# Two cross-attentions whose maxima enter the score product, in a fused two-layer decoder

## What is computed

```
scores = einsum('nqhd,nkhd->nhqk', q, k)        # layer 1: divided by sqrt(16)
attn = softmax(scores, axis=3)
out = einsum('nhqk,nkhd->nqhd', attn, v) @ W + b
```

## Time and profile before

| | us |
|---|---|
| median of 3 runs (2005.93 to 2014.84) | 2013.31 |
| the profiled execution, its own time | 2014.15 |
| its span in the trace | 2012.2 |
| TensorE busy (matmul) / weight loads | 1711.1 (85%) / 1349.4 (67%) |
| VectorE / ScalarE / GpSimd busy | 1163.6 (58%) / 622.9 (31%) / 895.1 (44%) |
| mean granted clock of TensorE, share of full | 0.91 |
| layer 0 attention, first product to first shared unit | 27.49 to 577.18 |
| shared units and experts of layer 0 | 577.18 to 1146.9 |
| layer 1 attention to first expert tile | 1146.9 to 1590.5 |
| experts of layer 1 | 1590.5 to 2012.2 |

### The profile page before, as it was taken

The page is one execution under the profiler, slowest core; times in us unless marked ns, Lnnn a source line. Parts: engine busy times, 40 slices in busy tenths (PEclk is TensorE's granted clock), DMA queues, the critical chain, the costliest instruction groups (busy, mean ns, idle before and its releaser), DMA issues.

```text
span 2012.2 us, 45539 instructions
## 1 busy us (share of the span) xinstructions
PE 1711.1 (85%) x17739; PEld 1349.4 (67%) x17739; DVE 1163.6 (58%) x3228; ACT 622.9 (31%) x957; POOL 895.1 (44%) x1000
## 2 busy tenths in 40 slices
PE   3788888888789899998998478899987499999994
PEld 2676666666656566665666345676656499999994
DVE  3576655755532176776656456787765345665554
ACT  0233222332221176544455123354432011111110
POOL 0006557556758201888888856333322201222223
PEclk9999978988679999999999678999887699999997
DMA  9415434545457899987999922113101512333332
GB/s 320 147 36 195 161 133 159 171 145 173 164 171 215 224 289 299 297 271 252 296 299 305 301 78 83 54 65 129 63 33 50 169 49 75 92 95 93 101 92 69
DMA packets 269634, 322.61 MB, mean 160 GB/s; under 512 B 25083, under 2 KB 245487, under 8 KB 268655
## 3 DMA queue, kind: packets, MB, share of 16 engines
q1 hardware_dynamic: 236399, 227.38, 35.7%
q0 software_dynamic: 33024, 92.32, 14.1%
HBM read 157.22 MB, written 162.40 MB: 159 GB/s over the span
## 4 chain that ended last, share of the span: by engine, by line
PE 60%; DVE 11%; POOL 8%; issue 7%; DMA 5%; ACT 3%; another core or an unknown queue 3%; SPq 1%; DVEq 1%; POOLq 0%; ACTq 0%
PE wide L2039 13%; PE d_yp L2051 6%; POOL big L1413 5%; PE wide L1171 4%; PE wide L1174 3%; PE wide L110 3%; PE wide L127 3%; PE bank L1191 3%; PE wide L1158 2%; PE bank L1184 2%; PE bank L1005 2%; PE bank L1148 2%; ACT pt L650 2%; PE bank L1077 2%
## 5 line engine op out<-in xcount | busy, mean ns | idle before, releaser
L1413 POOL DMA_INDIRECT big<-results,slots x256 | 268.4, 1048 | 207.0 <-DMA results<-e_y 127.3
L2039 PE MATMUL wide<-d_xt,d_ws 128*128 128x128 f32 x2272 | 278.4, 276 | 0.6 <-issue 0.6
L2039 PEld LDWEIGHTS wide<-d_xt,d_ws 128*128 128x128 f32 x2272 | 272.1, 193 | 4.5 <-issue 1.0
L588 POOL DMA_INDIRECT lists<-big,slots x160 | 159.1, 994 | 118.5 <-DVE slots L940 72.1
L650 ACT ACTIVATE pt<-wide 77x2048 f32<-77x2048 f32 x64 | 119.9, 1873 | 210.9 <-PE wide L1174 126.7
L1908 POOL DMA_INDIRECT d_picked<-results,slots x64 | 63.8, 997 | 181.5 <-DMA results<-d_y 168.2
L1939 ACT ACTIVATE d_gate<-wide 128x512 f32<-128x512 f32 x71 | 42.4, 597 | 324.6 <-PE wide L2039 320.0
L1428 DVE SCALAR_TENSOR_TENSOR big<-big,weights 128x256 f32<-128x256 f32 x256 | 108.9, 486 | 51.9 <-DMA big<-results,slots 33.9
L2051 PE MATMUL d_yp<-d_wd,d_h 128*128 x568 | 134.2, 379 | 0.0
L110 PE MATMUL wide<-shared_sx,shared_sw 128*128 128x512 f32 x256 | 127.0, 619 | 6.3 <-DMA shared_sx<-res_t 3.8
L127 PEld LDWEIGHTS wide<-shared_sw,shared_sh 128*128 128x128 f32 x512 | 99.8, 196 | 46.3 <-issue 29.9
(11 more groups left out here) (280 smaller groups left out, 3528.3 us busy)
## 6 DMA issues: line engine op xcount, KB each, us to landing
lists<-zero SPq DMA_DIRECT2D x20, 2048.0 KB, 14.4
e_x<-lists SPq DMA_DIRECT2D x80, 512.0 KB
results<-e_y SPq DMA_DIRECT2D x80, 512.0 KB
d_x<-lists SPq DMA_DIRECT2D x71, 128.0 KB
results<-d_y SPq DMA_DIRECT2D x71, 128.0 KB
e_w<-in_L_w SPq DMA_DIRECT2D x2, 4096.0 KB
x<-in_x SPq DMA_DIRECT2D x8, 512.0 KB
shared_sw<-in_x_t SPq DMA_DIRECT2D x32, 128.0 KB
```

What stands on the lines that cost most here:

```text
L588: pool.indirect_dma_start(out=lists, out_offset=bass.IndirectOffsetOnAxis(ap=slots[:, b, i, k:k + 1], axis=0), in_=z2[i % 3][:, b, :], in_ ...
L1413: pool.indirect_dma_start(out=picked[:, c % NG, b, :], out_offset=None, in_=results[0:-(-PAGES_OF_STEP[s] // 4) * 4 * R0, :], in_offset=ba ...
L2039: ins = mm(out[T % 2][:, a * P:(a + 1) * P], ws[:, T % NW, n, c, a * P:(a + 1) * P], xt[:, T % 2, c], start=c == 0, stop=c == KC - 1)
```

## The change

1. The maxima are laid out differently. peak is now [128, batch, chunk, 128], and the negated maximum of a head stands in the column of one channel of the *other* head of its pair. mt has two jobs a step (a pair of batches each) of four transposes; their result has the maxima in rows that the masked copy of the queries leaves at zero.
2. ScalarE makes, beside the plain copy of the transposed queries (x1t in layer 0, q in layer 1; semaphore qt_done), two masked copies `split[:, a]` with mask2 as scale. VectorE's part of mt adds the maxima into the other rows of each: `split = maxima * mask2[other] + split`.
3. keys_max is a second set of keys with ones (sel_at) added in the row of the maxima. sc is one product, keys_max x split, where it was two. `sel` is gone; mx keeps keys and the plain queries.
4. SEQUENCE0 and SEQUENCE1 are new orders, with other distances between stages (in layer 0 v, kt, ret, mix, mx, sc, x2t one round later relative to qk, for instance; b2's halves in two rounds).
5. Layer 0: x_t is loaded first, then eight constants on their own semaphore consts_soon, then x and the rest. TensorE starts after consts_soon; it waits for the others before ("wo", 0, 0) and for the tables (READY, now 31) before ("mx", 0, 0). VectorE makes the retention's tables first and the others (`lay_out`) when it reaches ("mx", 0, 0). Layer 1: context, wk and wv are loaded first, and ten loads (`others`) are issued from ScalarE's queue; the tables are still made before the first job.

```
-SEQUENCE0, stages in the order before: wo, wo, put, v, v, ln1, wout, wout, cwt, put, qk,
-  x1t, x1t, mx, ln2, qk, b2, b2, mx, res, put, qk, x2t, x2t, mx, put, qk, mx, put, kt, ret, kt, put, mt, rt, put, put,
-  sc, mix, top, ret, pv, sc, mix, up, rank, sc, pv, sc, pv, pv
+SEQUENCE0 = [
+    ("mx", 2, 1), ("x1t", 2, 1), ("put", 4, 2), ("up", 2, 0), ("mx", 2, 2), ("b2", 4, 1), ("v", 1, 0), ("mx", 2, 3),
+    ("kt", 1, 0), ("mt", 2, 0), ("ret", 1, 0), ("ln2", 3, 0), ("mt", 2, 1), ("v", 1, 1), ("x2t", 3, 0), ("x2t", 3, 1),
+    ("ret", 1, 1), ("kt", 1, 1), ("rt", 3, 0), ("put", 4, 3), ("put", 4, 4), ("top", 3, 0), ("mix", 1, 0), ("put", 4, 5),
+    ("mix", 1, 1), ("put", 4, 6), ("wo", 1, 0), ("wo", 1, 1), ("put", 4, 7), ("rank", 3, 0), ("res", 2, 0), ("cwt", 3, 0),
+    ("qk", 0, 0), ("sc", 2, 0), ("qk", 0, 1), ("sc", 2, 1), ("pv", 2, 0), ("sc", 2, 2), ("qk", 0, 2), ("pv", 2, 1),
+    ("sc", 2, 3), ("pv", 2, 2), ("pv", 2, 3), ("b2", 3, 0), ("wout", 2, 0), ("ln1", 1, 0), ("put", 3, 0), ("x1t", 1, 0),
+    ("wout", 2, 1), ("put", 3, 1), ("mx", 1, 0), ("qk", 0, 3),
+]
+SEQUENCE1 = [
+    ("mx", 3, 0), ("wout", 4, 0), ("mx", 3, 1), ("wout", 4, 1), ("num", 2, 0), ("num", 2, 1), ("lqk", 1, 0), ("mx", 3, 2),
+    ("sig", 1, 0), ("lv", 1, 0), ("up", 2, 0), ("ln2", 4, 0), ("mt", 3, 0), ("mx", 3, 3), ("ct", 2, 0), ("tri", 1, 0),
+    ("tri", 1, 1), ("x2t", 4, 0), ("wo", 2, 0), ("wo", 2, 1), ("x2t", 4, 1), ("sc", 3, 0), ("rt", 4, 0), ("mt", 3, 1),
+    ("sc", 3, 1), ("top", 4, 0), ("pv", 3, 0), ("ln1", 2, 0), ("sc", 3, 2), ("put", 5, 0), ("pv", 3, 1), ("x1t", 2, 0),
+    ("x1t", 2, 1), ("rank", 4, 0), ("pv", 3, 2), ("sc", 3, 3), ("q", 2, 0), ("q", 2, 1), ("pv", 3, 3), ("x0t", 0, 0),
+    ("kvt", 1, 0), ("x0t", 0, 1),
+]
...
         if first:
+            loads = [loads[1]] + others[1:] + [context]
+            others = []
+            soon = [(wv[:], col(d["wv"])), (wqk[:, :, 0:DM], col(d["wq"])), (wqk[:, :, DM:], col(d["wk"])),
+                    (scale_qk[:, 0:2], d["decay_q"]), (decay_s[:], d["decay_s"]), (block_mask[:], d["block_mask"]),
+                    (causal[:], d["causal"]), (ident[:], d["ident"])]
...
             begin_here(sp)
+            load_t(0)
+            for dst_ap, src_ap in soon:
+                sp.dma_start(dst_ap, src_ap).then_inc(consts_soon, 16)
             load(0)
-            load_t(0)
...
+                    if stage == "x1t" and first:
+                        nc.scalar.activation(out[:, :, cols].rearrange("p c (b n) -> p b c n", b=2), turned_rows, ACT.Copy)\
+                            .then_inc(qt_done, 1)
+                        for a in range(2):
+                            ins = nc.scalar.activation(split[:, a, :, cols].rearrange("p c (b n) -> p b c n", b=2), turned_rows,
+                                                       ACT.Copy, scale=mask2[:, a:a + 1])
+                        empties(ins, job)
...
-                if stage == "mt":
-                    move(peak_t[:], filled(act, job)[:], job)
...
+                        make(nc.vector.tensor_scalar(keys_max[:, b, :, h * CTX:(h + 1) * CTX], kin, mask2[:, h:h + 1],
+                                                     sel_at[:, 1 - h:2 - h], ALU.mult, ALU.add))
...
+                if stage == "mt":
+                    ps = filled(dve, job)
...
+                    for a in range(2):
+                        half_of = split[:, a, :, p * 2 * P:(p + 1) * 2 * P]
+                        ins = nc.vector.scalar_tensor_tensor(out=half_of, in0=ps[:].rearrange("p (c n) -> p c n", c=KC),
+                                                             scalar=mask2[:, 1 - a:2 - a], in1=half_of, op0=ALU.mult,
+                                                             op1=ALU.add)
+                    empties(ins, job)
...
                 if stage == "mt":
-                    emptied(pe, ("mx", i, NB - 1))
-                    for b in range(NB):
-                        ins = tr(out[:, toks(b)], peak[:, b], ident[:])
+                    emptied(pe, ("mx", i, 2 * p + 1))
+                    for bb in range(2):
+                        for c in range(KC):
+                            ins = tr(out[:, (c * 2 + bb) * P:(c * 2 + bb + 1) * P],
+                                     peak[:, 2 * p + bb, c], ident[:])
                     fills(ins, job)
                 if stage == "sc":
-                    emptied(pe, ("mt", i, 0))
+                    emptied(pe, ("mt", i, p // 2))
...
                         for r in range(4):
-                            mm(out[0:CTX, r, n * P:(n + 1) * P], keys[quarter(r), p, c, h * CTX:(h + 1) * CTX],
-                               qt[quarter(r), c, toks(p)], start=True, stop=False, skip_group_check=True)
-                        for r in range(4):
-                            ins = mm(out[0:CTX, r, n * P:(n + 1) * P], sel[quarter(r), n], peak_t[quarter(r), toks(p)],
-                                     start=False, stop=True, skip_group_check=True)
+                            ins = mm(out[0:CTX, r, n * P:(n + 1) * P], keys_max[quarter(r), p, c, h * CTX:(h + 1) * CTX],
+                                     split[quarter(r), h, c, toks(p)], start=True, stop=True)
```

More of the change, by code:

```diff
@@ L261, in attention_phase @@
         mask2 = sb("mask2", [P, 2])
-        sel_at = sb("sel_at", [P, 4])
-        sel = sb("sel", [P, 4, CTX])
+        sel_at = sb("sel_at", [P, 2])
         causal = sb("causal", [P, P])
         keys = sb("keys", [P, NB, KC, 2 * CTX])
+        keys_max = sb("keys_max", [P, NB, KC, 2 * CTX])
         vals = sb("vals", [CTX, NB, XH, 2 * XD])
@@ L368, in attention_phase @@
         consts = sem("consts")
+        consts_soon = sem("consts_soon") if first else None
         ready = sem("ready")
@@ L375, in attention_phase @@
         x1_done = sem("x1_done")
+        qt_done = sem("qt_done")
         att_done = sem("att_done")
@@ L557, in _ @@
             nc.gpsimd.memset(eps[:], LN_EPS).then_inc(pool_ready, 1)
-            nc.gpsimd.memset(peak[:], 0.0).then_inc(pool_ready, 1)
+            nc.gpsimd.memset(units.sh[:], 0.0).then_inc(pool_ready, 1)
             if first:
@@ L608, in _ @@
             begin_here(act)
+            for dst_ap, src_ap in others:
+                act.dma_start(dst_ap, src_ap).then_inc(consts, 16)
             if not first:
-                act.wait_ge(consts, 16 * len(loads))
+                act.wait_ge(consts, CONSTS)
                 nc.scalar.activation(small[:, 0:1], gate[:], ACT.Exp, scale=-1.0).then_inc(gate_exp, 1)
@@ L614, in _ @@
                 pair = slice(2 * p, 2 * p + 2)
+                if first and job == ("x1t", 0, 0):
+                    act.wait_ge(ready, READY)
                 if stage == "unit":
@@ L644, in _ @@
                 if stage == "q":
-                    move(qt[:, p], filled(act, job)[:], job)
-                if stage == "mt":
-                    move(peak_t[:], filled(act, job)[:], job)
+                    ps = filled(act, job)
+                    nc.scalar.activation(qt[:, p], ps[:], ACT.Copy).then_inc(qt_done, 1)
+                    for a in range(2):
+                        ins = nc.scalar.activation(split[:, a, p], ps[:], ACT.Copy, scale=mask2[:, a:a + 1])
+                    empties(ins, job)
                 if stage == "sc":
@@ L711, in _ @@
             make(nc.vector.memset(vals[:], 1.0))
-            dve.wait_ge(consts, 16 * len(loads))
-            make(nc.vector.tensor_reduce(mask2[:], head_mask[:].rearrange("p (m h) -> p h m", h=2), AX.X, ALU.add))
-            make(nc.vector.tensor_reduce(sel_at[:], ident[:].rearrange("p (r n) -> p n r", r=4)[:, 0:4], AX.X, ALU.add))
-            make(nc.vector.tensor_copy(sel[:], sel_at[:].unsqueeze(2).broadcast_to([P, 4, CTX])))
-            make(nc.vector.memset(ones_row[:], 1.0))
-            make(nc.vector.memset(base[:], 0.0))
-            make(nc.vector.memset(counts[:], 0.0))
             if first:
+                dve.wait_ge(consts_soon, 16 * len(soon))
                 make(nc.vector.reciprocal(scale_qk[:, 2:4], scale_qk[:, 0:2]))
@@ L752, in _ @@
+            if not first:
+                lay_out()
             for job in order:
                 stage, i, p = job
+                if first and job == ("mx", 0, 0):
+                    lay_out()
                 if stage == "late":
@@ L971, in _ @@
             begin_here(pe)
-            pe.wait_ge(consts, 16 * len(loads))
-            if not first:
+            if first:
+                pe.wait_ge(consts_soon, 16 * len(soon))
+            else:
+                pe.wait_ge(consts, CONSTS)
                 for b in range(NB):
@@ L982, in _ @@
                     fills(ins, ("key", b, 0))
-            pe.wait_ge(ready, READY)
             if first:
                 pe.wait_ge(state_done, 1)
+            else:
+                pe.wait_ge(ready, READY)
             for job in order:
                 stage, i, p = job
+                if first and job == ("wo", 0, 0):
+                    pe.wait_ge(consts, CONSTS)
```

(2 more changed lines are left out.)

123 lines of the change are left out of this document (65 added, 58 removed), and 10 rows, old and new, of tables (SEQUENCE0, SEQUENCE1).

## The result

| measured session | chip | kernel before, median us | this kernel, median us | ratio, 95% interval |
|---|---|---|---|---|
| first comparison, changed kernel | not recorded | 2012.47 (4 runs) | 2053.51 (2050.85 to 2066.06, 4 runs) | 1.0222 [1.0184, 1.0261] |
| the changed kernel once more (after_again) | 8 | 1878.85 (13 runs) | 1859.43 (1855.37 to 1865.77, 4 runs) | 0.9895 [0.9855, 0.9936] |

The change is 2.2% slower where the prediction said 6.3% faster, and on another chip it is 1.0% faster. There are two kinds of chip here, as I take it: on those of the first kind the kernel before takes 2011 to 2026 us (the first comparison, chip 12 in two sessions, chip 14), on the second 1879 (chips 6 and 8, one session each). That it is the chip, and not something else that changes from session to session, is likely by chip 12 and not shown beyond it.

A forecast was written before the change was run, and what follows sets the result against it. The prediction took TensorE's strict order in layer 0, with refill waits and slow clock, as the bound; gains of 17 + 14 + 5 + 67 + 12 + 12 = 127 us from 2014 gave 1887 us, range 1848 to 1955.

The forecast's parts named there:

- The step that failed: Layer 0's steady loop: steps of 68.4 us were read as the 51.64 us step plus roughly 15 of slow clock.
- the forecast of 55: Layer 0's steady step in the new order: 55 us, 51 or so if the clock stays up, 62 if it falls.
- start: Start of layer 0: TensorE begins at 11 instead of 27.49, so wo(0) comes at 40, 17 us earlier.
- to wo(1): Stretch from wo(0) to wo(1): 27 of work and 8 of wait for tables, 35 us against 49.41, 14 less.
- to wo(2): Stretch from wo(1) to wo(2) in layer 0: 47 us against 51.64, 5 less.
- five steps of 55: Layer 0's five full steps: 275 us together against 341.9, 67 less.
- The end of layer 0: From wo(7) to the first shared unit: 65 us against 76.98, 12 less.
- Layer 1 and all behind it: Layer 1: its start and early steps gain nothing, five other steps 2.5 us each, 12 less.
- SyncE's order: Layer 0: the next step's x_t load queues behind a late wait; about 20 us of slack, so costed at nothing.
- the clock stays up: Rival, chance 0.27: layer 0's steps meet GpSimd's 51 us, end and layer 1 gain another 15, total 1852 us.
- The one that ended slower: Rival, chance 0.06: with half its sc work gone TensorE stays at low clock, layer 0 step 76 us, total 2036.
- the clock falls as before: Rival, chance 0.22: layer 0 step 62 us, its end 72, layer 1 gains 3, total 1938 us.

The follow-up runs named there:

- before_no_puts2: The kernel before without GpSimd's indirect puts of layer 0, steps 0 to 6, on chip 12: 1927.60 us (one run) beside 2011.32.
- no_puts: The changed kernel without GpSimd's indirect puts of layer 0, steps 0 to 6, on chip 12: 1878.86 us (one run).
- clears_late: The changed kernel with SyncE issuing a step's clears of the lists only after pv's last product, on chip 12: 2059.46 us, ratio 1.0167.
- before_no_puts: The kernel before without GpSimd's indirect puts of layer 0, steps 0 to 6, on chip 6: 1877.10 us (one run) beside 1878.99.

## Why the prediction was wrong

**The step that failed** is in the first part: "The slow step is thus the same step plus roughly 15 us of slow clock." The same steps without puts, at clock 0.97 to 1.00, take 54 to 55.6 us (before_no_puts2), so the 13 to 15 are right in size and wrong in cause: it is GpSimd's puts. The rows also didn't bear 15 us of slow clock: at 0.92 the step of 66.95 can hold 5.4 us of it and at 0.83 one of 70.6 some 12 (length times the missing share). I compared the step at 106.71 with the later ones as the same jobs plus b2 and cwt, and left out what starts in between on another engine: 32 puts, which I did look at the earlier trace rows, but as a floor of GpSimd's queue alone. With the clock as a cause of its own, the denser order was to give 13 us a step; the forecast of 55 rests on that. With the puts, what counts is which of TensorE's jobs they meet, and the new order puts the first twelve of a step onto sc(3) and two pv: steps of 80.6. They also come in one unbroken row there (372.07 to 387.99 in the step shown). In the kernel before they come in three groups of four with GpSimd's norms between: the first, for instance, at 292.38 beside the last pv and wo, the second at 305.81 beside wout, cwt and qk.

**The sum, term by term** (first comparison): start, 17 predicted and 25.7 measured (first product at 9.4 against 11, wo(0) at 31.6 against 40); to wo(1) 35 and 41.0, with a wait of 9.3 for the tables against 8; to wo(2) 47 and 46.55, so that at wo(2) the changed kernel stood where predicted (122 and 119.1). Then five steps of 55 and 80.6: 67 us less became 61 more, 128 of the 166.5 us by which I was off. The end of layer 0: 65 and 101.0. Even on a chip where the puts cost nothing it is 74.9, since the rounds are turned and more of a step's work now lies behind wo(7); that term was mis-sized by 10 for this reason, and by 26 for the puts. Layer 1 and all behind it: 12 predicted and 46 - 37 = 9 measured, and that is luck. The gain of 5.6 us from sc(0) to sc(7) (308.9 before, 303.3 now) is there because the kernel before is slowed more on this chip than the changed one (on chip 8 they take 269.4 and 293.8); on chip 8 the term would have had the wrong sign.

**By part.** Where no put holds it, the sc job is 1.04 us from its start to the next job (0.95 predicted from 1.91 and 0.96). The multiply-add took 0.742 (0.75). The reduce kept 1.43. VectorE, ScalarE and GpSimd have the work predicted (44.3, 20.5 and 41 a step). SyncE's order, costed at nothing, was right: no wait of TensorE for a DMA of x_t stands in the step at 360.42. On the second kind a step is 49.6 to 52, at 0.97 to 1.00 in the two shown, which is the case "the clock stays up" (51). The gain there is small because the kernel before has no slow steps either (54.5 us), because the end of layer 0 is 74.9 against 53.0, and because layer 1 loses 24.

**The rivals.** The one that ended slower named the wrong cause (the clock, with half of the sc work gone): no_puts has that same work at clock 0.94 to 1.00. Its number, 2036, was near for another reason. The clock did fall, to 0.79 to 0.83, as the rival "the clock falls as before" said, but not by the mix of jobs: no_puts has the same transposes at 0.94 to 1.00. So the rule of the Trainium skill that I set beside it (TensorE: Matmul & The Clock Gate, Part 4: PE-mode transpose) doesn't explain the slow steps.

**Layer 1 on the second kind** stays open. TensorE loses 17 us in those 294 to waits for VectorE's `turned` (L882), and VectorE's work is 22 us more than before (246.6 against 224.8), 3.1 a step, which is what mt was costed at. The columns are us in total, times, and the longest; in the changed kernel:

```profile
PE bank L1230 <- DVE turned L882: 10.5, 5, 2.1
PE bank L1191 <- issue: 8.5, 5, 2.7
PE wide L1205 <- DVE shared_sh L864: 7.9, 8, 2.3
...
PE bank L1237 <- DVE turned L882: 5.3, 2, 3.9
PE wide L1220 <- DVE shared_sx L876: 1.7, 1, 1.7
PE bank L1128 <- DVE turned L882: 1.3, 1, 1.3
```

TensorE waits for mt itself (`shared_sx`) only 1.7 us. This is read from the trace, and no run on this kind of chip separated the order from mt.

## What to carry to other kernels

When one step of a loop is slow and its twin is not, list what begins on every engine and queue between the two before blaming the clock; then take that thing out in one run. Multiply out what the clock can cost (length times the missing share) before it is made the cause. Idle time of TensorE called "issue" inside a job is the sign of something outside the job: TensorE waits there for nothing in the program, and what helped was moving the other engine's work (2004.62 us by one wait on GpSimd). Measure on more than one chip before an order is called better: this one is 2.2% slower on one kind and 1.0% faster on the other.

## What the runs showed of the hardware

On chips 12 and 14, beside GpSimd's indirect DMAs of 128 rows (0.96 us of its queue, one each 1.27), TensorE's stream of short products comes in bursts of some four records per 1.4 us with unexplained idle time between; on chips 6 and 8, with the same program, it doesn't. Taking layer 0's out gives 84 us in the kernel before (2011.3 to 1927.6, chip 12) and some 180 in the changed one (2059 to 1879, both on chip 12, by clears_late, which is as slow as the changed kernel); each number without puts is a single run. The granted clock falls with them (0.79 to 0.83, and 0.94 to 1.00 without). The loss doesn't depend on the bytes moved, nor on how full the DMA engines are (0.24 or 0.40 of them). Jobs of a few long records mostly kept their length (qk, four records, 1.91 us at 374.56 with puts beside it; wo, 3.56 in four of the five slow steps of the kernel before and 5.1 in one); sc(3) grew from 1.04 to between 7.7 and 13.2 us and mix from 3.6 to between 6.9 and 9.3; but ret, with 32 short records, stayed at 1.1 (in the kernel before its second job grew to between 1.8 and 3.2). What in GpSimd's work reaches TensorE, why two kinds of chip differ, and how much of the 35 us that the kernel before loses in layer 1 on chip 12 (307.0 against 271.6 from sc(0) to sc(7), before_no_puts2 and before_no_puts) is due to the puts there, no run shows.
